# Stacked single-pass products for eight of ten mixes, the diagonal of the recurrence as one sum per head, and the rows of ones loaded ahead of the second stacks

## The reference, cut to what matters

```python
xx = shift(x) - x                                  # token before, minus this token
lora = jnp.tanh((x + xx * maa_x) @ maa_w1).reshape(B, T, 5, 32)
m = jnp.einsum('btfd,fdc->fbtc', lora, maa_w2)     # the five "mixes", 32 -> 256
xf = x + xx * (maa_f + m[f])                       # f = w, k, v, r, g
r, k, v = xr @ Wr, xk @ Wk, xv @ Wv
g = jnp.tanh(xg @ gate_w1) @ gate_w2
wdec = jnp.exp(-jnp.exp(time_decay + jnp.tanh(xw @ decay_w1) @ decay_w2))
# per head of 64 channels, over the tokens:
y_t = r_t @ (S + u * outer(k_t, v_t));   S = wdec_t * S + outer(k_t, v_t)
out = groupnorm(y) * g @ Wo
```

## Time and profile before

| | before |
|---|---|
| median of 3 runs | 3254.19 us (3253.11 to 3262.6) |
| the profiled execution | 3255.01 us |
| its span, first to last instruction | 3253.2 us |
| PE busy | 2884.9 us, 89% of the span |
| DVE / ACT / POOL busy | 2408.4 / 1314.2 / 1454.2 us |
| granted TensorE clock, mean | 0.961 |

### The profile page before, as it was taken

The page is one execution under the profiler, slowest core; times in us unless marked ns, Lnnn a source line. Parts: engine busy times, 40 slices in busy tenths (PEclk is TensorE's granted clock), DMA queues, the critical chain, the costliest instruction groups (busy, mean ns, idle before and its releaser), DMA issues.

```text
span 3253.2 us, 46577 instructions
## 1 busy us (share of the span) xinstructions
PE 2884.9 (89%) x16832; PEld 1771.7 (54%) x16832; DVE 2408.4 (74%) x4601; ACT 1314.2 (40%) x2753; POOL 1454.2 (45%) x1643
## 2 busy tenths in 40 slices
PE   4589989999898998989889898898989989899898
PEld 2236664456644576345763557635565355753567
DVE  7576788667786687866878668786687776877666
ACT  1373234632256323653136531374314732247322
POOL 2134562345524465244643446334462345623454
PEclk7799999999999999999989999999999999999999
DMA  7500043000520015000340002400024000240000
GB/s 160 111 2 1 20 71 69 2 10 14 83 53 2 11 30 91 29 2 10 49 99 2 2 20 40 99 2 2 20 40 99 2 1 20 40 86 2 1 1 14
DMA packets 70483, 114.97 MB, mean 35 GB/s; under 512 B 9323, under 2 KB 62603, under 8 KB 64059
## 3 DMA queue, kind: packets, MB, share of 16 engines
q1 hardware_dynamic: 66963, 110.72, 17.1%
q10 hardware_dynamic: 3264, 0.79, 0.1%
HBM read 74.69 MB, written 33.65 MB: 33 GB/s over the span
## 4 chain that ended last, share of the span: by engine, by line
PE 52%; DVE 22%; POOL 13%; issue 6%; ACT 3%; DMA 2%; SPq 1%; DVEq 0%; POOLq 0%; ACTq 0%
PE PB L1510 7%; PE PB L1425 6%; PE PB L1411 6%; PE PB L1441 6%; PE PB L1525 5%; DVE mxp L1094 5%; DVE arena L1280 4%; PE PB L1565 3%; DVE arena L1289 3%; PE PB L1600 3%; POOL rstd L572 2%; PE PB L1590 2%; DVE attn L997 2%; PE PB L1362 2%; POOL arena L704 2%
## 5 line engine op out<-in xcount | busy, mean ns | idle before, releaser
L1094 DVE TENSOR_REDUCE mxp<-PB 128x1 f32<-128x512 f32 (+3 forms) x1216 | 723.8, 652 | 145.5 <-PE PB L1414 79.8
L824 ACT ACTIVATE arena<-PB 128x512 f32<-128x512 f32 (+3 forms) x1536 | 658.6, 511 | 402.2 <-PE PB L1425 353.8
L1411 PE MATMUL PB<-arena 96*128 96x512 bf16 (+3 forms) x1536 | 463.2, 344 | 48.7 <-DMA arena<-parts 31.0
L1425 PE MATMUL PB<-arena 99*128 99x512 bf16 (+3 forms) x1536 | 445.0, 335 | 64.1 <-DMA arena<-augT 39.2
L675 POOL TENSOR_TENSOR hl<-arena,hh 128x512 fp32r<-128x512 f32 x192 | 251.8, 1315 | 293.4 <-ACT hh L851 291.8
L1441 PE MATMUL PB<-arena 128*32 128x512 f32 (+3 forms) x3072 | 326.5, 499 | 8.5 <-POOL arena L651 8.5
L1411 PEld LDWEIGHTS PB<-arena 96*128 96x128 bf16 x1536 | 151.4, 100 | 280.6 <-ACT arena L824 94.8
L695 POOL TENSOR_TENSOR arena<-arena,xT 128x512 f32<-128x512 f32 x160 | 184.3, 1176 | 261.7 <-DVE arena L1222 261.7
L651 POOL TENSOR_SCALAR_AFFINE_SELECT arena<-arena 128x512 f32<-128x512 f32 x256 | 162.7, 638 | 306.8 <-ACT arena L824 279.5
L1425 PEld LDWEIGHTS PB<-arena 99*128 99x128 bf16 x1536 | 139.2, 99 | 284.1 <-DVE mxp L1094 83.5
L1510 PE MATMUL PB<-xh,wgu 128*128 128x512 f32 x768 | 258.2, 418 | 29.5 <-issue 26.2
(11 more groups left out here) (142 smaller groups left out, 5418.6 us busy)
## 6 DMA issues: line engine op xcount, KB each, us to landing
arena<-parts SPq DMA_DIRECT2D x112, 256.0 KB, 9.3
parts<-arena SPq DMA_DIRECT2D x192, 128.0 KB
arena<-parts SPq DMA_DIRECT2D x16, 768.0 KB, 17.1
arena<-in_x SPq DMA_DIRECT2D x16, 512.0 KB, 7.2
arena<-parts SPq DMA_DIRECT2D x16, 512.0 KB, 19.4
xres<-in_x SPq DMA_DIRECT2D x16, 512.0 KB, 4.5
out<-xres SPq DMA_DIRECT2D x16, 512.0 KB, 13.3
wgu<-arena SPq DMA_DIRECT2D x2, 768.0 KB, 25.5
```

The costliest lines, as they stand in the source:

```text
L824: act.activation(pt[:, U % 3, h, 0:n], bank(b, "score", t)[:, 0:n], ACT.Exp, scale=DH ** -0.5).then_inc(act_emptied, 1)
L1094: dve.reduce_max(mxp[:, k // 2 % 2, hs[0]:hs[-1] + 1, col:col + 1], bank(b, "max", t)[:, 0:n * len(hs)].rearrange("p (h n) -> p h n", n=n) ...
L1411: last = mm(ps, qst[0:AUG, i // 4, HG * (k // 2) + h, 128 * (i % 4):128 * (i % 4) + 128], kst[0:AUG, s0 // HALF, HG * (k // 2) + h, 0:n], ...
L1425: mm(ps[:, 0:n], kst[0:AUG + 3, j // 4, h, 128 * (j % 4):128 * (j % 4) + 128], qst[0:AUG + 3, f, h, HALF - n:HALF], start=True, stop=True) ...
```

## The change

**Mixes.** Two of the ten mixes of a batch, (0, 0) and (0, 1), stay as they were. For the other eight, ACT makes `lora_hi`, a copy of lora rounded to fp32r (three copies a batch: f = 0, and f = 1 for both halves of the rows), and DVE makes `lora_lo` = lora - lora_hi. SP then builds for each mix a stack of 96 rows, hi, lo, hi, by three transfers of 32 rows x 512 inside SBUF. The weights `mw2s` are hi, hi, lo in the same 96 rows; DVE makes them once, in batch 0. The mix is then two fp32r matmuls.

**Diagonal.** ACT copies r a second time, into `rk` (the place of lora); DVE multiplies it by k (`weigh`, once for each half); PE multiplies it by `usel`, which holds u in one column for each of two heads: 16 matmuls of 2 columns, all into one bank. ACT copies the 32 sums for each token out (`dsum`) and makes A's 32 blocks as the identity times a scale for each partition. ku, the eight banks, their masked copies and the zeroing of A go.

**Ones.** The transfer of the rows of ones stands ahead of the nine of the second stacks.

```diff
+WHOLE = 2
-        add(b, "diag", range(8), "dve")
+        add(b, "diag", (0,), "act")
...
+        rk = lora
+        dsum, usel = region(HIGH + 13312, 32), region(HIGH + 13344, 4).rearrange("p (c h) -> p c h", c=NC)
+        lora_hi = [rounded(f"lora_hi{l}", HIGH + 12288 + 512 * l, [128, 1, HALF]) for l in (0, 1)]
+        lora_lo = [rounded(f"lora_lo{l}", 9728 + 1024 * l, [128, 1, HALF]) for l in (0, 1)]
+        mix_in = {(f, mi): rounded(f"mix_in{f}{mi}", at, [96, 1, HALF]) for (f, mi), at in stack_at.items()}
...
 stack_loads:
+            if m:
+                sp.dma_start(kst[AUG:AUG + 3, :, :, :], ones_dram).then_inc(ones_loaded, 16)
             for run, (first, n) in enumerate(RUNS):
...
-            if m:
-                sp.dma_start(kst[AUG:AUG + 3, :, :, :], ones_dram).then_inc(ones_loaded, 16)
...
 SP, in each batch, ahead of parts_store(b + 1, range(4)):
+                    for (f, mi), t_ in mix_in.items():
+                        fi = MIX_ORDER[mi]
+                        l, r = (0, 32 * fi) if fi < 4 else (1, 96)
+                        sp.wait_ge(lora_low, 3 * b + 1 + f + f * l)
+                        for k, part in enumerate((lora_hi, lora_lo, lora_hi)):
+                            sp.dma_start(t_[32 * k:32 * k + 32, 0, :].bitcast(f32),
+                                         part[l][r:r + 32, 0, :].bitcast(f32)).then_inc(mix_ready[f, mi], 16)
...
 POOL:
-                    pool.memset(A, 0.0).then_inc(a_zeroed, 1)
...
 ACT, lora_out:
+                            if n == 2:
+                                for mi in range(WHOLE, NMIX):
+                                    act.wait_ge(mix_ready[0, mi], 48 * (b + 1))
+                            if n != 1:
+                                p = slice(96 * l, 128)
+                                wait_emptied(act, b, "lora", n)
+                                act.activation(lora_hi[l][p, 0, :], lora[p, l, HALF * f:HALF * f + HALF],
+                                               ACT.Copy).then_inc(lora_high, 1)
 ACT, r_out:
+                            act.activation(rk[:, c, HALF * f:HALF * f + HALF], bank(b, "r", n)[:, :],
                                            ACT.Copy).then_inc(act_emptied, 1)
 ACT, behind v_out(1):
+                    wait_filled(act, b, "diag", 0)
+                    act.activation(dsum, bank(b, "diag", 0)[:, 0:32], ACT.Copy).then_inc(act_emptied, 1)
+                    wait_emptied(act, b, "diag", 0)
+                    for k in range(2 * NT):
+                        for h in (0, 1):
+                            last = act.activation(A[:, k // NT, k % NT, h, :], ident[:, :], ACT.Copy,
+                                                  scale=dsum[:, 2 * k + h:2 * k + h + 1])
+                        last.then_inc(diag_set, 1)
...
 DVE, in batch 0:
+                            for w2, fs in w2_in:
+                                dve.tensor_copy(mw2s[:, fs, :], w2).then_inc(s_cast, 1)
+                            for w2, fs in w2_in:
+                                dve.tensor_tensor(mw2s[64:96, fs, :], w2[64:96, :, :], mw2s[64:96, fs, :].bitcast(f32),
+                                                  ALU.subtract).then_inc(s_cast, 1)
...
+                    def lora_rest(n):
+                        dve.tensor_tensor(lora_lo[l][p, 0, :], lora[p, l, cols], lora_hi[l][p, 0, :].bitcast(f32),
+                                          ALU.subtract).then_inc(lora_low, 1)
+                    def weigh(f):
+                        for n in (2 * f, 2 * f + 1):
+                            a = rk[:, n % 2, HALF * f:HALF * f + HALF]
+                            wait_emptied(dve, b, "k", n)
+                            dve.tensor_tensor(a, a, kk[:, n % 2, HALF * f:HALF * f + HALF], ALU.mult).then_inc(rk_done, 1)
...
                     ln_means(2, b, 1, stats, mv)
+                    lora_rest(0)
...
                     mixed(3)
+                    lora_rest(2)
+                    lora_rest(3)
...
                     mixed(7)
+                    weigh(0)
                     mixed(8)
...
-                    for c in range(NC):
-                        wait_emptied(dve, b, "k", 2 + c)
-                        dve.tensor_scalar(ku[:, c, :], kk[:, c, :], vec[:, 7, c:c + 1], None, ALU.mult).then_inc(ku_done, 1)
-                    dve.wait_ge(a_zeroed, b + 1)
-                    for n in range(8):
...
-                        dve.copy_predicated(a, dmask[:, :].rearrange("p (a t) -> p a t", a=1).broadcast_to([128, 4, 128]),
+                    weigh(1)
...
-                                    wait_emptied(dve, b, "diag", 7)
+                                    dve.wait_ge(diag_set, 2 * NT * b + 4 * (2 * c + q) + 4)
...
 PE, mix_item:
-                        mm(bank(b, "mix", n)[:, :], mw2[:, fi, 128 * co:128 * co + 128],
-                           lora[:, fi // 4, HALF * f:HALF * f + HALF], start=True, stop=True).then_inc(filled, 1)
+                        if f == 0 and mi < WHOLE:
+                            last = mm(bank(b, "mix", n)[:, :], mw2[:, mi, cols], lora[:, fi // 4, 0:HALF], start=True, stop=True)
+                        else:
+                            pe.wait_ge(mix_ready[f, mi], 48 * (b + 1))
+                            last = mm(bank(b, "mix", n)[:, :], mw2s[:, fi, cols], mix_in[f, mi][:, 0, :], start=True, stop=True)
 PE, diag:
-                    for n in range(8):
...
-                                      ku[:, c, 128 * ch:128 * ch + 128], qd[:, c, :, 128 * ch:128 * ch + 128],
+                    for f in (0, 1):
+                        for c in range(NC):
+                            pe.wait_ge(rk_done, 4 * b + 2 * f + c + 1)
+                            for ch in range(4 * f, 4 * f + 4):
+                                last = mm(bank(b, "diag", 0)[:, 2 * (NT * c + ch):2 * (NT * c + ch) + 2],
+                                          rk[:, c, 128 * ch:128 * ch + 128], usel[:, c, :], start=True, stop=True)
```

More of the change, by code:

```diff
@@ L339, in build @@
         S = region(HIGH + 12288, 1024).rearrange("p (c n j) -> p c n j", c=NC, n=NT)
[L340 removed]
+        assert HIGH + 13348 <= LAST
         zT = xT[:, :, 1:1 + T]
@@ L397, in build @@
         xxx_done = sem("xxx_done")
+        lora_high = sem("lora_high")
+        lora_low = sem("lora_low")
+        mix_ready = {key: sem(f"mix_ready{key[0]}{key[1]}") for key in stack_at}
         mix_added = sem("mix_added")
@@ L530, in _ @@
                 load(mw1[:, :, :], b_mat[4].rearrange("(c p) n -> p c n", p=128))
-                for f in range(NMIX):
+                for mi in range(WHOLE):
+                    f = MIX_ORDER[mi]
                     r = 32 * f if f < 4 else 96
-                    load(mw2[r:r + 32, f, :], b_mat[5][f, :, :])
+                    load(mw2[r:r + 32, mi, :], b_mat[5][f, :, :])
+                for r in (0, 32, 64):
+                    for w2, fs in w2_in:
+                        load(w2[r:r + 32, :, :], b_mat[5][fs, :, :].rearrange("f r n -> r f n"))
                 load(low1[:, :, 0:DLOW], b_mat[6].rearrange("(c p) n -> p c n", p=128))
@@ L1225, in mixed @@
                                                      op0=ALU.add, op1=ALU.mult).then_inc(dve_emptied, 1)
+                    def lora_rest(n):
+                        l, f = n % 2, n // 2
+                        p, cols = slice(96 * l, 128), slice(HALF * f, HALF * f + HALF)
+                        dve.wait_ge(lora_high, 3 * b + 1 + (n - 1 if f else 0))
+                        if n == 2:
+                            for mi in range(WHOLE, NMIX):
+                                dve.wait_ge(mix_ready[0, mi], 48 * (b + 1))
+                        dve.tensor_tensor(lora_lo[l][p, 0, :], lora[p, l, cols], lora_hi[l][p, 0, :].bitcast(f32),
[5 more added lines that the diff above has]
+                            dve.tensor_tensor(a, a, kk[:, n % 2, HALF * f:HALF * f + HALF], ALU.mult).then_inc(rk_done, 1)
                     differences(0)
@@ L1563, in mix_item @@
                         wait_emptied(pe, b, "lora", 2 * f + 1)
+                        if n == 0 and b == 0:
+                            pe.wait_ge(s_cast, 5)
                         wait_bank(pe, b, "mix", n)
-                        mm(bank(b, "mix", n)[:, :], mw2[:, fi, 128 * co:128 * co + 128],
-                           lora[:, fi // 4, HALF * f:HALF * f + HALF], start=True, stop=True).then_inc(filled, 1)
+                        cols = slice(128 * co, 128 * co + 128)
+                        if f == 0 and mi < WHOLE:
[3 more added lines that the diff above has]
+                            last = mm(bank(b, "mix", n)[:, :], mw2s[:, fi, cols], mix_in[f, mi][:, 0, :], start=True, stop=True)
+                        last.then_inc(filled, 1)
                     def mix_items(f, mi):
@@ L1670, in _ @@
                     wait_emptied(pe, b, "r", 3)
-                    for n in range(8):
-                        c, q = n // 4, n % 4
-                        pe.wait_ge(ku_done, 2 * b + c + 1)
```

(12 more changed lines are left out.)

33 lines of the change are left out of this document (21 added, 12 removed).

## The result

The changed kernel takes 3181.1 us (median of 4 runs, 3171.1 to 3186.5), the kernel before 3253.7 beside it. The ratio is 0.9767, 95% interval 0.9751 to 0.9783: 72.6 us faster. 3167 was forecast, with 3142 to 3200 as the range. The profiled execution is the fastest of the four (3171.1 us, span 3169.0).

The account below looks back on a forecast made before the run. PE was taken to bound the mixes, a chain through DVE, POOL and PE the diagonal. 7 x (6.7 + 4.5) + 12.6 - 3.0 = 88.0 us; 3255.0 - 88.0 - 0.8 = 3166.2, said as 3167; range 3142 to 3200.

Parts of the forecast that it names:

- Mixes: Eight mixes on PE as fp32r pairs, 1.25 us saved each; next batch's q and k filled 6.7 us earlier.
- Diagonal: From the next batch's q fill to level 0 on DVE: 25.0 us becomes 20.5, 4.5 gained a batch (bounds 2 and 7).
- 32 blocks: ACT's scaled copies for A: 9.0 us in all (5.4 to 12), just hidden before DVE asks for them.
- The first stack of the second half: Before the second half's first stacked mix: ready about 1509.9, PE there at 1508.6, a wait of 1.3 us (0 to 4).
- It has to wait for DVE: Diagonal: PE finishes k and v at 12.5 us, DVE's low part comes at 14.4, so PE waits before the last tiny matmuls.
- the 3.8 us that the prediction worked out with it: Diagonal: by the exclusion rule each product of `weigh` takes 1.9 us, so this term is 3.8 instead of 3.1.
- Last batch: Batch with no q and k between: 4.1 us gained in the diagonal and 8.5 from the mixes, 12.6 in all.
- rival of the lost clock: PE's wait for `weigh` and the tiny matmuls put all seven levels at 1.2 GHz: 3367 us; slower had chance 0.04.
- A clock below 0.9 in the levels: Listed sign that the prediction is wrong: granted PE clock under 0.9 in the levels behind the diagonal.
- The argument against: Against the lost clock: the present diagonal holds full clock through waits of 1.2 and 0.4 us.
- level 1 and all behind it keep their instructions: Everything from level 1 on was taken as unchanged, with no term in the sum.
- The casts of batch 0: DVE rounds and subtracts weights once, some 2560 columns in attention: 3 us lost, between 0 and 9.5.

Follow-up runs that it names:

- e11_again: The changed kernel itself run once more, with nothing changed: median 3180.4 us, ratio 0.9773 to the kernel before.
- e8_stacks: The changed kernel with each of the 24 stack transfers of a batch made in two pieces of 16 rows: 3192.6 us, ratio 0.9811 to the kernel before.

## Why the prediction was right, and where its sizes were off

- **Mixes.** The mechanism was right: PE bounds this stretch. 6.7 us a batch for q and k were predicted; 6.6 are there with the mixes alone, 6.2 in the changed kernel, where PE waits 0.25 us for ACT's third copy of r. The waits that were foreseen, for POOL and for DVE's differences, came as 0.49 and 0.73 (0.4 and 1.0 predicted). The first stack of the second half was waited for 0.21 us instead of 1.3. DVE's subtraction ended 24.0 us behind lora, as worked out (23.9); but a transfer lands 2.0 us after the start of its issue, not 2.2 after the end, so the stack was there 0.6 us sooner, and PE asked for it 0.5 us later.
- **Diagonal.** From the rotary's first operation to level 0 on DVE are 24.7 us before and 19.7 after: 5.0 gained, 4.5 predicted, but by the wrong sum. "It has to wait for DVE" failed: DVE's low part was ready 13.1 us behind the rotary's start instead of 14.4 behind the fill, `weigh(1)` took 1.90 us instead of 3.1, and PE never waited. All 16 small products lay on the path, 3.7 us instead of 0.9, and the two level items took 3.6 instead of 1.8. The errors cancelled. Without the half clock the gain would have been 6.6. So the number was right by luck, the mechanism of this term was not.
- **DVE beside POOL.** `weigh(1)` took 1.90 us beside POOL's L737, the first pair 2.64 beside POOL's additions. The prediction took 1.9 for a product from L1035, which ran beside POOL's longest products of the decays; beside `weigh(1)` they were down to 256 and 128 columns:
```profile
1510.90 0.73 POOL L737 TENSOR_TENSOR arena<-arena 128x128 f32<-128x128 f32 x1
1511.29 0.88 DVE L1294 TENSOR_TENSOR arena<-arena 128x512 f32<-128x512 f32 x1
```
DVE's product ends at 1512.17, POOL's ended at 1511.63. The same 0.54 to 0.55 us lies between the two ends where a product or update of DVE in the recurrence (L1280; L1287, L1294, L1344) starts while one of POOL's runs, in 74 of 80 cases before (0.58 to 0.60 in the others) and in all 127 now: DVE waits for POOL's instruction to end, however long that is. The rule of "SBUF — State Buffer" (the Trainium skill, Who interferes with whom) is whole-instruction exclusion; the trace agrees, and the 3.8 us that the prediction worked out with it failed only because POOL's instructions were shorter than was taken.
- **ACT.** 9.46 us for 32 blocks against 9.0, and the 9.4 worked out from "ScalarE: Activation LUTs" of the Trainium skill: the trace agrees. Hidden, with 2 us to spare.
- **Last batch.** 12.6 predicted, 68.7 - 55.9 = 12.8 measured, 11.7 in e11_again; the mixes alone give 8.5, as predicted, the diagonal alone 3.2 instead of 4.1.
- **Clock.** The prediction gave its sum no term for the clock; its rival of the lost clock named the wait for `weigh` and the tiny matmuls, and feared for all seven levels. The wait did not come, the small products bring the clock down, and for level 0 alone. It cost 1.4 us a batch, 11 in all. "A clock below 0.9 in the levels" stood there as a sign of being wrong; it came, and the forecast held all the same. The argument against, full clock in the present diagonal, looked too short a way: 4 us behind it the kernel before ran at 0.68 in most batches, and its levels were the shorter for it.
- **The rest of the kernel.** This is the term that was mis-sized. The stretches gave 604.4 - 514.1 = 90.3 us, against 91.0 predicted (78.4 + 12.6). But 7.7 us came back between level 0 and the next lora, where 0 was written because "level 1 and all behind it keep their instructions". They do, but not their overlap: 4.8 us of it (6.3 of 7.0 in e11_again) are DVE's updates that now meet POOL's in the levels. Of the remaining 3.0 and 0.6 us the cause is open; PE's waits for issue are 9.8 and 6.6 us longer and those for augT 0.8 and 3.5, more than is missing. The casts of batch 0 were put at 3: the first lora starts at 291.8 to 294.5 us in the three without them and at 294.0 to 299.6 in the ten executions with them, 4.3 us later in the mean. The profiled execution is 84 us shorter; the median run is ten longer than that one. What makes it so is open: e11_again, 5 us longer than the first profiled execution, starts its first lora 4.4 us later.

## What to carry to other kernels

When a stage is replaced by many very small matmuls, price them by their distance (0.23 us a pair of records, as if they had 128 columns) and look at the granted clock of what follows: here widening them, or putting real work between, cost nothing and gave 11 us. Before a product on DVE is priced, look at what POOL runs beside it and for how long; an engine that becomes faster can move the two onto each other. A sum can come out right with two of its terms wrong; it is the waits, and who waits for whom, that say whether the working was right. And a saving in one stretch of a long hand-ordered kernel is partly returned by the stages around it, so read the stretch and the whole apart.

## What the runs showed of the hardware that was not expected

- A stretch of 3.7 us with 32 records of 128 x 2 columns is followed by a granted clock of 0.57 (3.6 us; 0.50 to 0.67 in the eight batches); 128 x 104 columns in the same time leave it at 1.00 in all eight.
- A wait of PE of 2.1 us was followed by a low clock (0.67 to 0.76 in the next 6 us) in four of seven batches of e8_stacks.
- A DVE product or update with both inputs in SBUF that starts while such a product of POOL runs ends 0.54 to 0.55 us behind it (201 of 207 cases in two traces): a lone update takes 0.69 us, one beside POOL's 1.45 us takes 1.67.
- Low clock on PE in one level made the levels shorter, 40.6 us instead of 41.5, because it kept POOL's update off DVE's.
- Products of 2 and of 104 columns with 128 x 128 float32 weights take the same time, 0.23 us for each pair of records.
- A copy on ACT with a scale from memory comes every 0.29 us at 128 columns and every 0.24 us at 64.
- A transfer of 64 KB from SBUF to SBUF lands 2.0 us after its issue; in two pieces of 32 KB it is later by the further issues, 1.9 us for three.
